# Audio tower with routed experts: the routing chain of the first expert slots, interleaved by hand on VectorE, and a new order of its work on TensorE and ScalarE

## What is computed

```python
logits = xf @ Wg                                  # xf: 2048 x 256, Wg: 256 x 8
top_w, top_i = jax.lax.top_k(logits, 2)
top_w = jax.nn.softmax(top_w, axis=-1)
one_hot = jax.nn.one_hot(top_i, 8)
combine = jnp.einsum('nk,nke->ne', top_w, one_hot)
h = jnp.einsum('nc,ech->enh', xf, W1)
g = jnp.einsum('nc,ech->enh', xf, W2)
y = jnp.einsum('enh,ehc->enc', silu(h) * g, W3)
out = jnp.einsum('enc,ne->nc', y, combine)
```

## Time and profile before

| | |
|---|---|
| median of three runs | 531.01 us (530.87 to 534.66) |
| the profiled execution | 533.95 us, of which the span is 532.2 |
| TensorE busy | 433.4 us (81%) |
| VectorE busy | 299.8 us (56%) |
| ScalarE busy | 206.6 us (39%) |
| GpSimd busy | 161.9 us (30%) |
| chain that ended last, by engine | TensorE 62%, VectorE 16%, DMA 7%, issue 7%, ScalarE 5% |

### The profile page before, as it was taken

The page is one execution under the profiler, slowest core; times in us unless marked ns, Lnnn a source line. Parts: engine busy times, 40 slices in busy tenths (PEclk is TensorE's granted clock), DMA queues, the critical chain, the costliest instruction groups (busy, mean ns, idle before and its releaser), DMA issues.

```text
span 532.2 us, 9176 instructions
## 1 busy us (share of the span) xinstructions
PE 433.4 (81%) x3291; PEld 282.8 (53%) x3292; DVE 299.8 (56%) x855; ACT 206.6 (39%) x385; POOL 161.9 (30%) x140
## 2 busy tenths in 40 slices
PE   0699897996767746546679999999799999999991
PEld 0254454654565535445436766676466666566661
DVE  0598875686889899988796388437231111111110
ACT  0235645255457324236223553345122332233321
POOL 6041010020111213431142536442443442455322
PEclk9999998999958956866779999999899999999997
DMA  9999010063180100822011422152223226232311
GB/s 181 249 214 203 19 29 2 20 210 133 36 297 29 46 2 2 293 102 80 0 43 27 119 31 50 28 133 30 43 37 51 39 41 195 39 59 40 49 20 20
DMA packets 36102, 43.14 MB, mean 81 GB/s; under 512 B 5216, under 2 KB 30560, under 8 KB 35904
## 3 DMA queue, kind: packets, MB, share of 16 engines
q1 hardware_dynamic: 26384, 32.14, 21.6%
q0 software_dynamic: 7488, 10.23, 12.1%
q10 hardware_dynamic: 2192, 0.27, 0.5%
HBM read 30.96 MB, written 11.53 MB: 80 GB/s over the span
## 4 chain that ended last, share of the span: by engine, by line
PE 62%; DVE 16%; DMA 7%; issue 7%; ACT 5%; SPq 1%; POOLq 0%; POOL 0%; DVEq 0%; ACTq 0%
PE psum L2095 22%; PE psum L2114 11%; PE psum L1746 8%; DMA KT<-in_L_attn_w_o_dram 3%; PE psum L2105 3%; PE psum L1785 3%; PE psum L1772 2%; PE psum L1760 2%; DMA out_dram<-mixture_rows_out 2%; PE psum L2085 1%; PE psum L1877 1%; DMA KT<-mixture_rows_in,src_i 1%; PE psum L1879 1%; DVE M2s L895 1%; DVE qtok L1142 1%
## 5 line engine op out<-in xcount | busy, mean ns | idle before, releaser
L1649 DVE TENSOR_TENSOR QT<-QT,psum 128x512 f32<-128x512 f32 x39 | 26.8, 688 | 136.7 <-PE psum L2095 136.5
L1746 PE MATMUL psum<-M2s,M1s 128*128 128x512 f32 x128 | 61.4, 624 | 20.0 <-DMA M1s<-in_L_tok_W_dram 18.2
L2095 PE MATMUL psum<-M1s,KT 128*128 x156 | 76.1, 611 | 1.5 <-ACT KT L806 1.0
L2114 PE MATMUL psum<-M3s,KT 128*128 x312 | 74.2, 381 | 1.5 <-ACT KT L814 0.8
L2095 PE MATMUL psum<-M2s,KT 128*128 x156 | 74.1, 598 | 0.0
L2114 PEld LDWEIGHTS psum<-M3s,KT 128*128 128x128 f32 x312 | 58.5, 190 | 22.0 <-issue 15.9
L825 ACT ACTIVATE O<-psum,gate_slot 128x256 f32<-128x256 f32 x39 | 18.5, 474 | 109.7 <-PE psum L2114 106.9
L504 POOL DMA_INDIRECT KT<-mixture_rows_in,src_i x39 | 41.0, 1052 | 45.0 <-issue 23.4
L2095 PEld LDWEIGHTS psum<-M2s,KT 128*128 128x128 f32 x156 | 30.1, 193 | 38.6 <-issue 38.6
L1746 PEld LDWEIGHTS psum<-M2s,M1s 128*128 128x128 f32 x128 | 24.0, 198 | 45.2 <-issue 25.7
L531 POOL DMA_INDIRECT mixture_rows_out<-O,src_i x17 | 31.4, 1848 | 33.3 <-ACT O L825 14.6
(11 more groups left out here) (398 smaller groups left out, 732.5 us busy)
## 6 DMA issues: line engine op xcount, KB each, us to landing
M3s<-in_x_dram SPq DMA_DIRECT2D x4, 1024.0 KB, 10.4
M3s<-in_L_ffn_W_dram SPq DMA_DIRECT2D x1, 4096.0 KB, 15.2
M2s<-in_L_ffn_W_dram SPq DMA_DIRECT2D x1, 4096.0 KB, 15.0
M1s<-in_L_ffn_W_dram SPq DMA_DIRECT2D x1, 4096.0 KB, 13.8
M3s<-in_x_dram SPq DMA_DIRECT2D x4, 992.0 KB, 14.1
M1s<-vtok SPq DMA_DIRECT2D x64, 34.0 KB, 1.9
mixture_rows_out<-H SPq DMA_DIRECT2D x4, 512.0 KB, 4.1
M1s<-in_L_tok_W_dram SPq DMA_DIRECT2D x2, 512.0 KB, 13.9
```

Of the source, the lines that this page charges most:

```text
L1649: v.tensor_tensor(sil[:, u, :], sil[:, u, :], bank[3], ALU.mult).then_inc(v_gated, 1)
L1746: last = mm(bank[6 + c], W1s[:, r, P * c:P * (c + 1)], xr[:, i % 2, r].rearrange("p b l -> p (b l)"), start=(n == 0), stop=(n == STRIDE - 1))
L2095: last = mm(z, xrT[:, u, c, :], w[:, bass.ds(e, 1), c, :].rearrange("p a h -> p (a h)"), start=(c == 0), stop=(c == CH - 1))
L2114: last = mm(bank[6][:, 0:DM], actT[:, u, c, :], M3s[:, bass.ds(e, 1), c, :].rearrange("p a d -> p (a d)"), start=(c == 0), stop=(c == HC - 1))
```

## The change

**VectorE.** `own()` can wait for one named pass instead of the latest. `ranks`, `full_blocks`, `positions`, `pair_slots`, `slots_hot`, `rows_of` and the seven gate passes of `gates_of` become one function for the first slots, `first_slots`, which puts the gate passes and `F_off` between passes that wait for each other. `whole` rounds in two passes (it adds and takes off 128 times the old constant), for all its callers. `F_at` comes from the running sum by another path with a new `F_skip`. `top_two` is split: `top_one` stands ahead of `att_norm2`, and its copy and first maximum both read PSUM and do not wait for each other. `rows_hot(0)` comes ahead of `table_tiles`. `token_of` is two passes instead of three (`tile_no` now holds the tile's first token number plus 128), and `slot_gates` one reduction instead of three passes. `state_re(2)` comes ahead of `top_expert(3)`; the two products of `state_turn(2)` (`state_angle`) move ahead of slot 0's gating, the sum (`state_sum`), `slot_gates(0)` and `used_blocks` stay or come behind it.

**TensorE.** `places2(0)` stands ahead of `norm2_columns(last)`; `slot_tables(0)` behind the first two of the four `expert_rows`; `slot_up(0)` ahead of `slot_rows(1)`. `norm2_columns` goes tile by tile and waits for ScalarE's rows one at a time, in all steps.

**ScalarE.** `gap_exp(1)` and `norm2_columns` come ahead of the copy of norm3; `table_rows(0)` behind the first copy of `expert_rows`; `gate_exp(3)` and the table load for Silu behind `slot_rows(0)`, and `slot_silu(0)` ahead of `slot_rows(1)`.

The core of the diff (left out: the gate passes as functions of one line each, the iota of `tile_no`, callers in the loop):

```diff
...
             act.wait_ge(p_scores, BT * STEPS)
             norm(SE, 2, N3_of[2], v_norm3_in, a_norm3)
             norm2_rows(STEPS - 1)
+            gap_exp(1, slice(0, EARLY))
+            norm2_columns(STEPS - 1)
             act.wait_ge(p_norm3T, 3)
             act.wait_ge(v_state_re, 2)
             act.wait_ge(g_input_im, 2)
             a.activation(xT3, banks(4), ACT.Copy).then_inc(a_norm3T, 1)
-            norm2_columns(STEPS - 1)
-            gap_exp(1, slice(0, EARLY))
-            expert_rows(STEPS - 1)
+            expert_rows(STEPS - 1, range(0, 1))
             table_rows(0)
-            gate_exp(3)
-            a.activation(silu_ready[:], row_p[:], ACT.Silu)
+            expert_rows(STEPS - 1, range(1, TS))
 
             def last_norm3():
...
@@ -826,8 +825,10 @@
                              ).then_inc(a_slot_out, 1)
 
             slot_rows(0, 0)
+            gate_exp(3)
+            a.activation(silu_ready[:], row_p[:], ACT.Silu)
+            slot_silu(0, 0)
             slot_rows(1, 1)
-            slot_silu(0, 0)
             for j in range(SLOTS):
                 u = j % 2
...
+                    state_angle(i)
+                state_sum(i)
+
+            def state_angle(i):
+
+                uRs = uR[i % 2]
+                dve.wait_ge(v_state_re, i + 1)
+                ln(v.tensor_tensor(cbl(uRs), cbl(uRs), tab(CT[:, :, 0:L]), ALU.mult))
+                dve.wait_ge(v_state_im, i + 1)
+                ln(v.tensor_tensor(cbl(uI), cbl(uI), tab(ST[:, :, 0:L]), ALU.mult))
+                own()
+
+            def state_sum(i):
+
+                uRs = uR[i % 2]
                 v.tensor_tensor(uRs, uRs, uI, ALU.add).then_inc(v_ssm_out, 1)
...
+            def top_one(lo, n, z):
+
                 ts = slice(lo, lo + n)
                 here = lg[:, ts, :]
-                ln(v.tensor_copy(here, z[:, 0:n * E].rearrange("p (t e) -> p t e", e=E)))
-                own()
-                best(here, rs[:, 0, ts], rs[:, 1, ts], ra[:, 0, ts], ra[:, 2, ts], ra[:, 3, ts])
+                fresh = z[:, 0:n * E].rearrange("p (t e) -> p t e", e=E)
+                ln(v.tensor_copy(here, fresh))
+                ln(v.tensor_reduce(rs[:, 0, ts], fresh, AX, ALU.max))
+                own()
+                chosen(here, rs[:, 0, ts], rs[:, 1, ts], ra[:, 0, ts], ra[:, 2, ts], ra[:, 3, ts])
+
+            def next_best(lo, n):
+
+                ts = slice(lo, lo + n)
+                here = lg[:, ts, :]
                 ln(v.scalar_tensor_tensor(ra[:, 4, ts], ra[:, 0, ts], -1e30, here, ALU.mult, ALU.add))
                 own()
...
             def ranks(lo, n, z):
 
-                ln(v.tensor_copy(ra[:, 7, lo:lo + n, :], z[:, 0:n * E].rearrange("p (t e) -> p t e", e=E)))
-                own()
+                return ln(v.tensor_copy(ra[:, 7, lo:lo + n, :], z[:, 0:n * E].rearrange("p (t e) -> p t e", e=E)))
 
             def whole(out, counts, half):
 
-                ln(v.tensor_scalar(out, counts, half, 1.0 / P, ALU.add, ALU.mult))
-                own()
-                ln(v.tensor_scalar(out, out, MAGIC, None, ALU.add))
-                own()
-                ln(v.tensor_scalar(out, out, MAGIC, None, ALU.subtract))
-                own()
-
-            def full_blocks(counts):
-
+                own(ln(v.tensor_scalar(out, counts, half, P * MAGIC, ALU.add, ALU.add)))
+                own(ln(v.tensor_scalar(out, out, P * MAGIC, 1.0 / P, ALU.subtract, ALU.mult)))
+
+            def first_slots(counts, n, ts):
+
+                copied = ranks(0, n, bank[2])
                 whole(F, counts, -(P - 1) / 2)
-                ln(v.tensor_tensor_scan(F_end, ones_e[:], F, 0.0, ALU.mult, ALU.add))
-                ln(v.tensor_scalar(F_lim, F, float(P), None, ALU.mult))
-                own()
+                ends = ln(v.tensor_tensor_scan(F_end, ones_e[:], F, 0.0, ALU.mult, ALU.add))
+                limit = ln(v.tensor_scalar(F_lim, F, float(P), None, ALU.mult))
+                limit1 = ln(v.tensor_scalar(F_skip, F, float(P), 1.0, ALU.mult, ALU.add))
+                own(limit)
+                out = ln(v.tensor_tensor(ra[:, 2, 0:n], ra[:, 7, 0:n], eb(F_lim, n), ALU.is_gt))
+                own(limit1)
+                at = ln(v.scalar_tensor_tensor(F_at, F_end, float(P), F_skip, ALU.mult, ALU.subtract))
+                own(out)
+                moved = ln(v.scalar_tensor_tensor(ra[:, 3, 0:n], ra[:, 2, 0:n], FAR, ra[:, 7, 0:n], ALU.mult, ALU.add))
                 ln(v.tensor_tensor(F_off, F_end, F, ALU.subtract))
-                own()
-                ln(v.tensor_scalar(F_at, F_off, float(P), -1.0, ALU.mult, ALU.add))
-                own()
+                own(moved)
+                placed = ln(v.tensor_tensor(ra[:, 4, 0:n], ra[:, 3, 0:n], eb(F_at, n), ALU.add))
+                dve.wait_ge(a_pair_gate, 1)
+                total = pair_total(ts)
+                own(placed)
+                pairs = ln(v.tensor_tensor(ra[:, 5:7, 0:n], ra[:, 0:2, 0:n], ra[:, 4:5, 0:n].to_broadcast([P, 2, n, E]),
+                                           ALU.mult))
+                own(total)
+                first = pair_first(ts)
+                own(pairs)
+                where = ln(v.tensor_reduce(rs[:, 5:7, 0:n], ra[:, 5:7, 0:n], AX, ALU.add))
+                own(first)
+                second = pair_second(ts)
+                own(where)
+                near = ln(v.tensor_scalar(slot_in[:, :, 0:n], rs[:, 5:7, 0:n], -(P - 1) / 2, P * MAGIC, ALU.add, ALU.add))
+                own(second)
+                high = gate_high(ts)
+                own(near)
+                slots = ln(v.tensor_scalar(slot_in[:, :, 0:n], slot_in[:, :, 0:n], P * MAGIC, 1.0 / P,
+                                           ALU.subtract, ALU.mult))
+                own(high)
+                left_over = gate_left(ts)
+                own(slots)
+                rows = row_in_slot(0, n)
+                slots_hot(0, n, FULL_EARLY, slot_in)
+                own(left_over)
+                mid = gate_mid(ts)
+                own(rows)
+                rows_hot(0)
+                table_tiles(0, n, FULL_EARLY)
+                own(mid)
+                low = gate_low(ts)
+                rows_hot(1)
+                own(low)
 
             def used_blocks():
...
             def token_of(z, lo, n):
 
-                tile1, row = z[:, 0:n], z[:, n:2 * n]
                 f = [src_f[:, k, lo:lo + n] for k in range(3)]
-                ln(v.tensor_scalar(f[0], tile1, float(P), -float(P), ALU.mult, ALU.add))
-                own()
-                ln(v.tensor_tensor(f[1], f[0], row, ALU.add))
-                own()
-                v.tensor_scalar(src_i[:, lo:lo + n], f[1], 0.0, None, ALU.max).then_inc(v_src, 1)
+                ln(v.tensor_reduce(f[1], z[:, 0:2 * n].rearrange("p (w s) -> p s w", w=2), AX, ALU.add))
+                own()
+                v.tensor_scalar(src_i[:, lo:lo + n], f[1], -float(P), 0.0, ALU.add, ALU.max).then_inc(v_src, 1)
...
             def slot_gates(which, lo, n, z):
 
                 dve.wait_ge(p_gate_table, which + 1)
-                g = gate_slot[:, lo:lo + n]
-                ln(v.tensor_copy(g, z[:, 0:n]))
-                own()
-                ln(v.tensor_tensor(g, g, z[:, n:2 * n], ALU.add))
-                own()
-                v.tensor_tensor(g, g, z[:, 2 * n:3 * n], ALU.add).then_inc(v_gate_slot, 1)
+                v.tensor_reduce(gate_slot[:, lo:lo + n], z[:, 0:3 * n].rearrange("p (m s) -> p s m", m=3), AX, ALU.add
+                                ).then_inc(v_gate_slot, 1)
...
             att_added(last)
             answered(later=1)
             minus_mean(SE, v_norm3_in)
+            dve.wait_ge(p_logits, 2)
+            top_one(0, EARLY, bank[2])
             att_norm2(last)
-            dve.wait_ge(p_logits, 2)
-            top_two(0, EARLY, bank[2])
+            next_best(0, EARLY)
             dve.wait_ge(p_places2, 1)
-            ranks(0, EARLY, bank[2])
-            full_blocks(bank[2][:, EARLY * E:(EARLY + 1) * E])
-            positions(EARLY, ALU.is_gt, F_lim, F_at)
-            pair_slots(EARLY)
-            slots_hot(0, EARLY, FULL_EARLY, slot_in)
-            table_tiles(0, EARLY, FULL_EARLY)
-            rows_of(0, EARLY)
-            rows_hot(0)
-            rows_hot(1)
+            first_slots(bank[2][:, EARLY * E:(EARLY + 1) * E], EARLY, slice(0, EARLY))
             full_experts(0, 0, FULL_EARLY)
             dve.wait_ge(p_table, 1)
             token_of(bank[3], 0, FULL_EARLY)
-            gates_of(1, slice(0, EARLY))
             gate_tables(0, EARLY, FULL_EARLY)
+            state_re(2)
             top_expert(3)
-            state_re(2)
             state_im(2)
-            slot_gates(0, 0, FULL_EARLY, bank[1])
-            used_blocks()
+            state_angle(2)
...
             for j in range(FULL):
                 slot_gate(j, j % 2)
                 if j == 0:
-                    state_turn(2)
+                    state_sum(2)
```

(9 more changed lines are left out.)

80 lines of the change are left out of this document (45 added, 35 removed).

## The result

The changed kernel takes 523.79 us (median of 4 runs, 523.38 to 525.4), against 532.8 for the kernel before, run beside it on the same chip (4 runs, 530.87 to 534.66): ratio 0.9851, 95% interval 0.9813 to 0.989. It is faster by 1.5%; I had forecast 527.4 with a range of 525.4 to 530.4, and called a change within 1% the likeliest. That is 6.3 less, where 3.6 were forecast. Two executions of 697 and 1134 us, whose cause is unknown, are left out of all means.

The account below looks back on a forecast made before the run. The prediction took the handover ahead of slot 0 through VectorE, then TensorE's slot loop, to bound the kernel. Slot 0's gating 3.4 earlier plus 0.2 at slot 17 gave 531.01 - 3.6 = 527.4 us, range 525.4 to 530.4.

Parts of the forecast that it names:

- Step 1: Places ahead of norm2's transposes on TensorE: VectorE has them at 252.3 in place of 254.91, 2.6 earlier.
- Step 2: VectorE's routing chain from the places' copy to the second rows_hot: 5.85 in place of 6.75, passes put between costing nothing.
- rival with fillers of 0.10 or 0.17 each: Passes put into VectorE's chain cost time: at 0.17 the kernel takes 527.9, at 0.10 TensorE hides it; chance 0.08.
- Step 3: Table products behind two gate rows: they start at 259.2, 3.1 earlier than 262.27, with TensorE the last ready.
- Step 4: From tables to slot 0's gating: VectorE takes 12.5, gating at 272.3, 3.4 earlier; TensorE's wait grows to about 2.0.
- rival that this gap takes the clock: TensorE's idle of some 2.0 before slot 0's gated rows lowers the clock, losing 1.8: 529.2; chance 0.25.
- Step 5: The rest: the loop passes 3.4 through unchanged, token_of saves 0.2 at slot 17, norm2's transpose order counts nothing.
- Sum: Whole kernel: 3.4 + 0.2 = 3.6 saved, carried over to the median, 531.01 - 3.6 = 527.4.
- more gain: More than forecast, by a clock that rises earlier in the gate rows or isn't lost at 382; chance 0.03.

Follow-up runs that it names:

- a_again: The changed kernel run again with no edit; mean 524.4 us, ratio 0.9864 to the kernel before.
- u_gates: The changed kernel with the seven gate passes back behind the token numbers on VectorE; mean 529.2 us.
- a_fetch: The changed kernel with ten products that nobody reads on TensorE in its wait for slot 0's fetched rows; mean 528.5 us.
- b_fetch: The kernel before with sixteen products that nobody reads on TensorE in its wait for slot 0's fetched rows; mean 531.5 us.
- a_third: The changed kernel run once more with no edit; mean 526.5 us, ratio 0.99 to the kernel before.
- a_best: The changed kernel with a_fetch's products, eight more in slot 17's wait, and state_turn(2) wholly behind slot 0's gating; mean 523.1 us with its repeat.
- a_angle_fetch: The changed kernel with a_fetch's products and state_turn(2) wholly behind slot 0's gating, without slot 17's products; mean 524.1 us.

## Why the prediction was wrong, point by point

- **Step 1, places 2.6 earlier: right.** Counted from the bias they are 2.8 earlier (6.73 before, 3.92 after; 2.5 in a_again).
- **Step 2, a chain of 5.85 with free fillers: right.** It takes 5.71. The rival with fillers of 0.10 or 0.17 each fell: the seven gate passes cost 0.17 in all, five of them nothing. The rule of the Trainium skill, "VectorE: DVE Perf Modes", section "The DRAIN you can't avoid", that the next pass doesn't start until the pipe is empty, would as I read it have the chain 1.2 longer for these seven; the trace doesn't agree for a pass that fits between two dependent ones. The section itself excepts a next pass that is not held, and with that the trace doesn't clash.
- **Step 3, tables 3.1 earlier with TensorE last: right in kind.** It is 3.6 in the first profile after (14.09 to 10.45), 2.9 and 3.2 in the two others. In the first the clock rose at 254.7, 0.5 ahead of the tables; in a_again it rose only behind them.
- **Step 4, gating 3.4 earlier: right, a little small.** 4.2, 3.4 and 3.8 in the three profiles. VectorE needs 12.28 from tokens to gating (12.51 forecast, the difference being `state_angle`, 2.36 in place of 2.58), TensorE waits 1.40 for the gated rows (2.0 forecast). The rival that this gap takes the clock did not come true in the changed kernel; it did in u_gates and a_fetch.
- **Step 5: 0.2 at slot 17** is 0.1 (2.13 to 2.04). That norm2's order counts nothing was wrong: alone it is worth 2.3 to 2.4, of which the profiles show 0.6 to 1.1 at the gating. Beside step 1 the profile shows nothing of it, and the mean 2.3 with a standard error of 1.0.
- **Sum: this is the step that failed.** I added 3.6 of handovers and carried them over "a removed wait carries over" to the median, with the granted clock as it was and norm2's order at nothing. The handovers are worth 3.8 by the three profiles (27.56 to 23.75 in the mean from bias to gating). The mean fell by 6.3, so 2.5 lie outside them. The changed kernel also runs at a higher granted clock, 0.920 against 0.914, and by the line through all runs that goes with 2.5. The forecast named this only as 0.03 of chance for "more gain", while it gave 0.13 to a time below 525.7, and its range ended 2 below the forecast, though its own rows showed half clock at 382 and up products of 3.20 ahead of others of 1.88 at slot 0; step 4 took these 3.20 into the new kernel as a time of the work.
- **Where the 2.5 come from stays open.** Three places can be looked at. At slot 0 the half clock is 3.4 shorter in all profiles after, through the two gate rows in the fetch wait. That is 1.7 us of lost clock, which the line prices at 1.0; but b_fetch says that the kernel before gains nothing by this alone, and in the changed kernel VectorE is just as late. Behind slot 17's wait a stretch costs 1.7, and both profiles before have it and one of three after; but over all kernels it is as frequent without the change (3 of 5) as with it (6 of 11). Ahead of the bias, the stretch at 88 is in 3 of 6 profiles without and 3 of 14 with the change, at some 3 us each; no moved instruction stands ahead of it, and a_third has it, with the mean of its batch 2.3 above that of the other ten runs. The other candidate, norm2's order, has the right size in the means of three comparisons and no path in the changed kernel's profile. The runs don't part these.

## What to carry to other kernels

Where the trace shows the granted clock at its lower level, a forecast needs two sums: one of the waits, and one of the stretches at that level which the edit could shorten, move or make, each with its price and with how often it comes, since here 2.5 of 6.3 were in no sum of waits and went with the clock. Here work that was due anyway, put into a wait of TensorE, shortened the half clock as much as products that nobody reads did (6.8 to 3.4, by two gate rows or by b_fetch's sixteen products), and a shorter TensorE stretch pays only if the engine behind it isn't late as well: check both arrivals at the meeting point before moving either. And compare profiles from a common instruction ahead of the change, and several of them; a third of the difference between the two profiled spans was there before the change began.

## What the runs showed of the hardware

- Executions of one kernel differ by up to 6 us, within one batch on one chip too (528.8 to 534.9 before, with a mean granted clock of 0.922 and 0.903). A stretch at half clock around 88 to 95 us comes in six of twenty profiles; the last norm3's bias stands at 248.1 to 250.0 in these six and at 244.7 to 246.6 in the others, some 3 us sooner.
- Slot 17's wait was followed by 3.4 us of half clock in a_again, where it was 1.95 long, and not in the first profile after, where it was 2.04.
- TensorE kept busy through one wait moved the half clock to the next one: a_fetch, none at 262 to 266, then 3.4 behind an idle of 2.89. Only with both waits short (0.90 and 0.63 in a_best, 0.82 and 0.63 in a_angle_fetch) was there none at slot 0.
- VectorE passes of 8 to 128 elements a partition that wait for one another leave room for an independent one of 0.16 to 0.20 us at no cost (2.66 us without, 2.67 with five of them); between two passes that don't wait such a pass cost 0.08 (two of them in u_gates against the first profile after).
